# Context of chunks 1 to 3 loaded by columns and masked in place, in an attention and expert kernel on one core

## Chip, cores and metric

The kernel runs on one core of one Trainium2 chip. The metric is the device time of one execution in microseconds (us), lower is better; each kernel is run several times and the median counts.

## What is computed

One layer over 32 sequences of 64 tokens with 128 features, in fp32: cross-attention with 8 heads against a context, a small feed-forward part, and a mixture of 16 routed experts (the best 2 of 4 groups, then the best 4 experts) with two shared ones.

```python
q = einsum('bsd,hdk->bhsk', layernorm(x), Wq);  k = einsum('btd,hdk->bhtk', ctx, Wk);  v = ...(ctx, Wv)
A = m * (q @ k.T) + (1 - m) * -1e30;            o = softmax(A) @ v
y = layernorm(ctx + o @ Wo) * g0 + b0
x = x + layernorm(y + relu(y @ W1 + b1) @ W2 + b2) * g1 + b1'
h = layernorm(x)
combine = route(h @ router_w.T)                 # sigmoid, 2 groups of 4, 4 experts, weights normalised, x 2.5
out = x + sum_e combine_e * (silu(h @ gate_e) * (h @ up_e)) @ down_e + shared(h)
```

## The kernel before

The 2048 tokens are 16 tiles of 128, in four chunks (`c` = 0 to 3) of four tiles (512 tokens). Each engine has its own list of pieces (`key(c, h)`, `scores(n)`, `gate(n)`, ...), written out by hand as calls. The engines run their lists in that order and meet only at semaphores, so the order of the calls is the schedule. From `up(42)` on the lists are loops.

Wq and Wk of each head are folded into one matrix at the start (`fold` on PE, `centre` and `fold_low` on DVE, `fold_high` on ACT). What was folded is then multiplied by the context. `key(c, h)` makes the keys of chunk `c` and head `h` with three single-pass matmuls of 128x512: the operands are split into a high part (a copy rounded to fp32r) and a low part (the residue), and high x high, high x low and low x high are added in PSUM. Of the context, chunk `c` therefore needs features on partitions, times the mask, split in two:

- `mask_context(c)` (POOL, lines 430 to 440) multiplies the context by rows, `ctx_all`, by the mask of each token into `ctx_m`;
- `turn_ctx(c)` (PE, lines 1498 to 1507) turns the four tiles of `ctx_m` with transposes into PSUM bank `key_bank[0]`;
- `cT_high(c)` (ACT) casts the bank to `cT_hi`, `cT_low(c)` (DVE) takes bank minus `cT_hi` into `cT_lo`;
- then `key(c, 0)` to `key(c, 7)`, whose results ACT copies to `k_T` (`key` on ACT).

`scores(n)` multiplies a tile of x by the keys (bank 4), DVE applies mask and scale (`mask`, `maximum`), POOL subtracts the maximum, ACT takes the exponent, DVE sums, POOL normalises, `turn_probs` and `spread` turn the probabilities, `attend` multiplies the context by them, `heads_out` copies, `project` applies the folded Wv and Wo, and `add_ctx` adds the context. `turn_x1`, `ffn_up`, `ffn_down` are the feed-forward part of a chunk, `turn_xm` and `route` its router logits.

The routing is done in two halves of eight tiles. DVE works from `bias_scores` to `combine`; `turn_combine` turns the weights on PE, `take_combine` copies them, SP stores them to DRAM and loads each expert's row, broadcast to 128 partitions. `weigh(n)` on POOL multiplies an expert's activations by it. `up(n)` is six matmuls (gate and up, three each) for step `n`, that is one expert and one chunk; `down(n)` adds its result to the chunk's sum in PSUM. The first weighted step is 4.

All large loads but the first ones are issued by SP in one queue (lines 332 to 361): x of chunk 0, context of chunk 1, `mask_add` (the additive mask, two transfers of 256 KB), the second half of the attention weights, `ctx_swap`, the remaining rows and columns of x and the context, small weights, and, once the folds are done, the gate and up weights in three batches and the down weights. PSUM bank 0 serves `turn_ctx` and the even heads, counted by `key_use` and `ctx_use`.

Of the kernel before, what the change touches and what calls it, by code (L numbers as in the profile page):

```python
# [57 lines left out]
def build(nc, x, x_cols, ctx_in, mask_tok, mask_pairs, w_attn, w_gu, w_dn, small, w1, w2, vec, out):  # L58
    es = ExitStack()
    with es:  # L60
# [23 lines left out]
        ctx_m = sb("ctx_m", [P, TPC, P])  # L84
        mask_col = sb("mask_col", [P, NT])
# [114 lines left out]
        ld_c0, ld_c1, ld_c = sem("ld_c0"), sem("ld_c1"), sem("ld_c")  # L200
        ld_mask_col, ld_mask, ld_swap0, ld_swap = sem("ld_mask_col"), sem("ld_mask"), sem("ld_swap0"), sem("ld_swap")
# [17 lines left out]
        cT_hi_ready = sem("cT_hi_ready")  # L219
# [26 lines left out]
        def ctx_use(c):  # L246

            return c * (1 + HP) + 1

        def key_use(c, h):  # L250

            return ctx_use(c) + 1 + h // 2 if h % 2 == 0 else c * HP + h // 2 + 1

# [65 lines left out]
        def _(sp):  # L319
# [15 lines left out]

            sp.wait_ge(ld_w[0][1], 16)
            rows(0, 1, ld_x0)
            context(1, 2, ld_c1)
# [7 lines left out]
            columns(1, 2, ld_xt[1])  # L346
            context(2, CH, ld_c)
# [45 lines left out]
        def _(pool):  # L393
# [36 lines left out]
            def mask_context(c):  # L430

                if c < 3:
                    pool.wait_ge((ld_c0, ld_c1, ld_c)[c], 16)
                if c == 0:
                    pool.wait_ge(ld_mask_col, 16)
                else:
                    pool.wait_ge(key_full[0], ctx_use(c - 1))
                now = slice(c * TPC, (c + 1) * TPC)
                pool.tensor_tensor(ctx_m[:], ctx_all[:, now, :], mask_col[:, now].unsqueeze(2)
                                   .to_broadcast([P, TPC, P]), ALU.mult).then_inc(ctx_m_ready, 1)  # L440
# [70 lines left out]
            subtract_max(0)  # L511

            subtract_max(1)
            mask_context(2)
            normalise_probs(0)
            inverse_root(0, 1)
            normalise_probs(1)

            subtract_max(2)

            subtract_max(3)
            normalise_probs(2)
            add_beta(0)
            group_order()
            inverse_root(0, 2)
            normalise_probs(3)
            mask_context(3)

            subtract_max(4)

            subtract_max(5)
            normalise_probs(4)
            bias_row_2()

            subtract_max(6)
            split_lo(0)
            normalise_probs(5)
            add_beta(1)

            subtract_max(7)  # L540
            normalise_probs(6)
            inverse_root(0, 3)
            add_beta(2)
            inverse_root(1, 0)

            subtract_max(8)

            subtract_max(9)
            normalise_probs(7)
            add_b2(0)  # L550

            subtract_max(10)
            split_lo(1)
            normalise_probs(8)
            split_lo(2)
            inverse_root(2, 0)

            subtract_max(11)
            normalise_probs(9)
            inverse_root(3, 0)  # L560
            normalise_probs(10)
            add_beta(3)
            inverse_root(1, 1)

            subtract_max(12)
            normalise_probs(11)

            subtract_max(13)
            add_b2(1)

            subtract_max(14)
            normalise_probs(12)

            subtract_max(15)
            normalise_probs(13)
# [3 lines left out]
            split_lo(3)  # L579
            inverse_root(3, 1)  # L580
            split_lo(4)
            split_lo(5)
            inverse_root(1, 2)
            add_b2(2)
            dn_low(0)
            inverse_root(1, 3)
            split_lo(6)
            dn_low(1)
            inverse_root(2, 2)
# [5 lines left out]
            weigh(9)  # L595
            weigh(10)
            weigh(11)
            add_b2(3)
            weigh(12)
            weigh(13)  # L600
            weigh(14)
            weigh(15)
            inverse_root(3, 2)
            inverse_root(2, 3)
            weigh(16)
            weigh(17)
            weigh(18)
            weigh(19)
            weigh(20)
            dn_low(2)  # L610
            weigh(21)
            weigh(22)
            inverse_root(3, 3)
            weigh(23)
            weigh(24)
            split_lo(7)
            weigh(25)
            weigh(26)
            weigh(27)
            weigh(28)  # L620
# [3 lines left out]
            weigh(31)  # L624
            weigh(32)
            weigh(33)
            dn_low(3)
            weigh(34)
            weigh(35)
            weigh(40)  # L630
            weigh(41)
            weigh(42)
            weigh(43)
            weigh(44)
            weigh(45)
            weigh(46)
            weigh(47)
            weigh(48)
            weigh(49)
            weigh(50)  # L640
            weigh(51)
            weigh(52)
            weigh(53)
            weigh(54)
            weigh(55)
            weigh(56)
            weigh(57)
            weigh(58)
            weigh(59)
            weigh(60)  # L650
            weigh(61)
            weigh(62)
            weigh(63)
            weigh(64)
            weigh(65)
            weigh(66)
# [1345 lines left out]
```

## Time and profile before

| | us |
|---|---|
| median of 3 runs | 298.83 (298.77 to 298.99) |
| profiled execution | 299.21 |
| its span | 297.4 |
| PE busy | 284.9 (96%) |
| POOL busy | 182.9 (61%) |
| DVE busy | 179.6 (60%) |
| ACT busy | 161.7 (54%) |
| HBM read / written | 27.54 MB / 1.18 MB |

The span is the time from the first to the last instruction. PE's busy time counts matmuls, and their ends are modelled, so neighbours overlap a little; the chain of waits shows them end to start. The granted clock of PE was 0.998 over the execution. The loads fall in the first 33 us, in which the 16 DMA engines are busy nearly all the time from 14 us on.

### The profile page before, as it was taken

How to read it: one execution, taken by the hardware profiler on the slowest of the kernel's cores; microseconds unless marked ns; L12 is line 12 of the kernel's file. 1: busy time of each engine (PE TensorE's matmuls, PEld its weight loads, DVE VectorE, ACT ScalarE, POOL GpSimd, SP SyncE). 2: the span in 40 equal slices, each digit the busy share in tenths (PEclk: the TensorE clock that was granted, in tenths of full speed). 3: DMA queues.
4: the chain of work that ended last, by engine and by line, in shares of the span. 5: the costliest groups of instructions: out<-in, count | busy, mean ns of one | idle time of the engine just before them, and what ended most of it. 6: DMA issues, size and time to landing. Idle time of an engine off the chain costs nothing.

```text
span 297.4 us, 4503 instructions
## 1 busy us (share of the span) xinstructions
PE 284.9 (96%) x1427; PEld 206.9 (70%) x1427; DVE 179.6 (60%) x476; ACT 161.7 (54%) x298; POOL 182.9 (61%) x167
## 2 busy tenths in 40 slices
PE   2999999999999999999799999999999999999995
PEld 2756568757786787866666766767668888888882
DVE  0747855656755686796173427358965756566561
ACT  2555857574776677863342544573254564545541
POOL 2148686855576466342566966846706787877881
PEclk9999999999999999999999999999999999999999
DMA  6799300003000001101752432320045246334101
GB/s 210 244 361 297 128 0 3 0 2 100 7 2 0 3 1 57 51 0 45 264 185 82 141 124 90 129 83 3 1 151 193 90 141 210 116 100 142 71 2 71
DMA packets 9575, 29.01 MB, mean 98 GB/s; under 512 B 1232, under 2 KB 2256, under 8 KB 9424
## 3 DMA queue, kind: packets, MB, share of 16 engines
q1 hardware_dynamic: 8688, 27.15, 27.2%
q10 hardware_dynamic: 864, 1.57, 1.6%
q8 instruction: 12, 0.20, 0.3%
q14 instruction: 11, 0.09, 0.1%
HBM read 27.54 MB, written 1.18 MB: 97 GB/s over the span
## 4 chain that ended last, share of the span: by engine, by line
PE 86%; DVE 5%; DMA 4%; POOL 2%; issue 2%; ACT 0%; DVEq 0%; POOLq 0%
PE bank L1494 15%; PE bank L1495 15%; PE bank L1496 15%; PE bank L1573 10%; PE bank L1700 9%; PE bank L1561 6%; PE bank L1533 5%; PE bank L1542 3%; PE bank L1595 2%; PE bank L1602 2%; DMA k_T<-comb_dram 2%; POOL k_T L497 2%; DMA ctx_all<-in_ctx_in 1%; PE bank L1624 1%; DMA comb_dram<-comb_T 1%
## 5 line engine op out<-in xcount | busy, mean ns | idle before, releaser
L497 POOL TENSOR_TENSOR k_T<-x_T,k_T 128x512 f32<-128x512 f32 x64 | 94.0, 1475 | 44.8 <-DVE x_T L1274 34.7
L789 ACT ACTIVATE x_T<-bank 128x512 f32<-128x512 f32 x72 | 42.9, 597 | 68.4 <-PE bank L1496 68.3
L1274 DVE TENSOR_TENSOR x_T<-bank,x_T 128x512 f32<-128x512 f32 x64 | 44.1, 690 | 53.2 <-ACT x_T L789 29.5
L1494 PE MATMUL bank<-mT_hi,we_hi 128*128 128x512 f32 x144 | 62.5, 434 | 0.0
L1495 PE MATMUL bank<-mT_lo,we_hi 128*128 128x512 f32 x144 | 56.9, 395 | 0.0
L1496 PE MATMUL bank<-mT_hi,we_lo 128*128 128x512 f32 x144 | 56.8, 395 | 0.0
L1700 PE MATMUL bank<-k_T,w_in 128*128 128x512 f32 x78 | 36.6, 595 | 1.8 <-POOL k_T L497 1.8
L1494 PEld LDWEIGHTS bank<-mT_hi,we_hi 128*128 128x128 f32 x144 | 27.1, 188 | 9.1 <-issue 3.5
L1495 PEld LDWEIGHTS bank<-mT_lo,we_hi 128*128 128x128 f32 x144 | 27.1, 188 | 8.2 <-issue 2.9
L1573 PEld LDWEIGHTS bank<-vo,o_T 128*128 128x128 f32 x256 | 30.2, 192 | 2.3 <-issue 2.0
L1496 PEld LDWEIGHTS bank<-mT_hi,we_lo 128*128 128x128 f32 x144 | 27.0, 188 | 6.5
L1573 PE MATMUL bank<-vo,o_T 128*128 128x128 f32 x256 | 31.6, 276 | 0.0
L419 POOL TENSOR_TENSOR sc_m<-sc_m,nmax 128x512 f32<-128x512 f32 x16 | 17.1, 1070 | 15.1 <-DVE nmax L1130 15.1
L403 POOL TENSOR_TENSOR rstd<-var_eps,neg_half 128x4 f32<-128x4 f32 x12 | 12.4, 1032 | 21.9 <-DVE var_eps L1093 21.8
L720 ACT COPY o_T<-bank 128x512 f32<-128x512 f32 x32 | 17.9, 591 | 14.6 <-PE bank L1561 14.5
L1700 PEld LDWEIGHTS bank<-k_T,w_in 128*128 128x128 f32 x78 | 14.3, 190 | 13.8 <-issue 11.0
L1279 DVE TENSOR_TENSOR act_lo<-k_T,act_hi 128x512 fp32r<-128x512 f32 x33 | 22.8, 692 | 1.2 <-ACT act_hi L798 1.2
L691 ACT COPY k_T<-bank 128x512 f32<-128x512 f32 x32 | 18.5, 590 | 7.6 <-PE bank L1496 6.8
L798 ACT CAST act_hi<-k_T 128x512 fp32r<-128x512 f32 x33 | 20.2, 616 | 4.4 <-POOL k_T L497 2.4
L427 POOL TENSOR_TENSOR prob<-sc_m,rsum 128x512 f32<-128x512 f32 x16 | 16.7, 1046 | 7.2 <-DVE rsum L1137 5.9
L1123 DVE SCALAR_TENSOR_TENSOR sc_m<-bank,rstd_in,mask_add 128x512 f32<-128x512 f32 x16 | 11.9, 744 | 13.7 <-PE bank L1533 11.4
L1561 PE MATMUL bank<-prob_T,ctx_all 64*128 64x256 f32 x64 | 18.1, 402 | 0.0
(127 smaller groups left out, 488.1 us busy)
## 6 DMA issues: line engine op xcount, KB each, us to landing
k_T<-comb_dram SPq DMA_DIRECT2D x32, 512.0 KB, 3.7
w_in<-in_w_gu SPq DMA_DIRECT2D x3, 768.0 KB, 4.4
w_in<-in_w_dn SPq DMA_DIRECT2D x1, 1152.0 KB, 9.7
w_in<-in_w_attn ACTq DMA_DIRECT2D x4, 256.0 KB, 4.8
w_in<-in_w_attn SPq DMA_DIRECT2D x2, 512.0 KB, 7.5
ctx_swap<-in_ctx_in SPq DMA_DIRECT2D x2, 384.0 KB, 12.0
out_x<-ctx_all SPq DMA_DIRECT2D x3, 256.0 KB, 4.6
x_all<-in_x SPq DMA_DIRECT2D x2, 256.0 KB, 5.7
```

Source lines behind the costliest of these rows:

```text
L497: pool.tensor_tensor(act[n % 4], s_u[n % 2], comb[u % RING][:, c % 2 * CW:(c % 2 + 1) * CW], ALU.mult).then_inc(weighed_ready, 1)
L691: a.copy(k_T[c % 2][:, :, h, :], key_bank[i][:].rearrange("p (b s) -> p b s", s=SEQ)).then_inc(key_free[i], 1)
L789: a.activation(silu[n % 2], h_bank[n % 2][:], ACT.Silu).then_inc(silu_ready, 1)
L798: a.copy(act_hi[n % LAG][:], act[n % 4]).then_inc(act_hi_ready, 1)
L1274: v.tensor_tensor(into, u_bank[n % 2][:], silu[n % 2], ALU.mult).then_inc(s_u_ready, 1)
L1279: v.tensor_tensor(act_lo[n % LAG][:], act[n % 4], act_hi[n % LAG][:].bitcast(F32), ALU.subtract).then_inc(act_lo_ready, 1)
L1494: pe.matmul(dst, w_hi, m_hi, start=start, stop=False)
L1495: pe.matmul(dst, w_hi, m_lo, start=False, stop=False)
L1496: return pe.matmul(dst, w_lo, m_hi, start=False, stop=stop)
L1561: last = pe.matmul(o_bank[j][:].rearrange("p (h b s) -> p h b s", b=2, s=SEQ)[:, :, s, :], held[rows, n, :], prob_T[n % 2][rows, :, s, :], ...
L1573: last = pe.matmul(av_bank[:, 0:P], o_T[n % 2][:, h % 2, h // 2, :], vo[:, h, :], start=(h == 0), stop=(h == NH - 1))
L1700: pe.matmul(acc[c][:], dn[:, e, :], act[n % 4], start=start, stop=stop).then_inc(down_full, 1)
```

## The change

Chunk 0 is handled as before. For chunks 1 to 3 the host lays out the context a second time by columns (`ctx_cols`), and the mask as one row of 2048 (`mask_row`). SP loads for each of them 512 columns of the context into one tile `ctx_t` (256 KB) and the mask row, broadcast to 128 partitions, into `mask_r` (256 KB). `mask_context` multiplies `ctx_t` by `mask_r` in place; `cT_high` and `cT_low` read `ctx_t` instead of the bank. `turn_ctx(1)` to `(3)` are gone. The context by rows is still loaded for all chunks; chunk 1's comes later in the queue. A semaphore `cT_ready` frees `ctx_t` and `mask_r` for the next chunk, and SP waits for it before the loads of chunks 2 and 3.

Besides, the lists of all five engines are in another order. `mask_rows` stands ahead of `mask_context(1)` on POOL, most `turn_probs`, `attend` and `project` stand earlier, `attend(15)` stands between `turn_xm(1)` and `route(1)`, `project(15)` right behind `project(14)`, `up(5)` behind `turn_combine(0)`, `turn_combine(1)` behind `down(33)`, `combine(0)` and `combine(1)` one DVE piece or more earlier, and the loops start at step 42 on all engines, with `dn_high(4)` and `dn_low(4)` ahead of them. The core of the diff; of the lists only the parts on which the text below rests:

```diff
+        ctx_t, mask_r = sb("ctx_t", [P, CW]), sb("mask_r", [P, CW])
+        ld_cols = [None] + [sem(f"ld_cols{i}") for i in range(1, CH)]
...
+            def context_columns(c):
+
+                now = slice(c * CW, (c + 1) * CW)
+                if c > 1:
+                    sp.wait_ge(cT_ready, c - 1)
+                sp.dma_start(mask_r[:], mask_row[now].partition_broadcast(P)).then_inc(ld_cols[c], 16)
+                sp.dma_start(ctx_t[:], ctx_cols[:, now]).then_inc(ld_cols[c], 16)
+
             sp.wait_ge(ld_w[0][1], 16)
             rows(0, 1, ld_x0)
-            context(1, 2, ld_c1)
+            context_columns(1)
...
             columns(1, 2, ld_xt[1])
+            context(1, 2, ld_c1)
             context(2, CH, ld_c)
...
             sp.dma_start(small_T[:], small).then_inc(ld_small, 16)
+            context_columns(2)
             sp.wait_ge(fold_done, 6)
...
                     sp.dma_start(dn, w_dn).then_inc(ld_dn, 16)
+                    context_columns(3)
...
             def mask_context(c):
-                if c < 3:
-                    pool.wait_ge((ld_c0, ld_c1, ld_c)[c], 16)
-                if c == 0:
-                    pool.wait_ge(ld_mask_col, 16)
-                else:
-                    pool.wait_ge(key_full[0], ctx_use(c - 1))
...
+                if c:
+                    pool.wait_ge(ld_cols[c], 32)
+                    pool.tensor_tensor(ctx_t[:], ctx_t[:], mask_r[:], ALU.mult).then_inc(ctx_m_ready, 1)
+                    return
...
             mask_context(0)
+            mask_rows()
             mask_context(1)
             inverse_root(0, 0)
-            mask_rows()
...
-                a.copy(cT_hi, key_bank[0][:]).then_inc(cT_hi_ready, 1)
+                a.copy(cT_hi, ctx_t[:] if c else key_bank[0][:]).then_inc(cT_hi_ready, 1)
...
-                v.tensor_tensor(cT_lo[:], key_bank[0][:], cT_hi.bitcast(F32), ALU.subtract).then_inc(key_free[0], 1)
+                v.tensor_tensor(cT_lo[:], ctx_t[:] if c else key_bank[0][:], cT_hi.bitcast(F32), ALU.subtract
+                                ).then_inc(cT_ready if c else key_free[0], 1)
...
             def key(c, h):
...
-                if h < 2:
-                    pe.wait_ge(key_free[0], ctx_use(c))
+                if c and h < 2:
+                    pe.wait_ge(cT_ready, c)
...
             key(0, 7)
-            turn_ctx(1)
             fold(1, 0)
...
             turn_xm(1)
+            attend(15)
             route(1)
             project(14)
-            attend(15)
+            project(15)
+            turn_x1(2)
             up(2)
...
             ffn_up(2, 0)
+            ffn_up(2, 1)
+            up(4)
...
             down(1)
             down(2)
-            ffn_down(2)
-            up(4)
+            turn_combine(0)
+            down(3)
+            turn_x1(3)
             up(5)
-            turn_combine(0)
...
```

## Rows read from the trace of the kernel before

**Rows 1.** The page, first part: TensorE's busy time, share of the span, instructions.

```profile
PE 284.9 (96%) x1427; PEld 206.9 (70%) x1427; DVE 179.6 (60%) x476; ACT 161.7 (54%) x298; POOL 182.9 (61%) x167
```

**Rows 2.** Waits of PE: waiter, what it waited for, total us, times, longest.

```profile
PE bank L1506 <- POOL ctx_m L439: 5.7, 1, 5.7
PE bank L1700 <- POOL k_T L497: 1.8, 1, 1.8
PE bank L1624 <- ACT xm_T L752: 0.7, 1, 0.7
PE bank L1652 <- DVE comb_w L1254: 0.6, 1, 0.6
```

**Rows 3.** Chain that ended last: start us, us, engine, tile, line, instructions.

```profile
16.64 0.64 PE bank L1506 x4
...
20.77 1.01 PE bank L1533 x4
...
28.50 0.44 PE bank L1506 x4
...
33.37 1.06 PE bank L1561 x8
...
45.78 1.79 PE bank L1573 x16
...
49.77 1.98 PE bank L1573 x16
```

**Rows 4.** Busy time by stretch: us, PE, PEld, DVE, ACT, POOL, clock, DMA share, GB/s.

```profile
22.00:24.00 2.00, 2.00 (x14) 1.79 (x14) 1.93 (x4) 1.10 (x2) 0.60 (x1) 1.00 1.07 259
...
28.00:30.00 2.00, 2.00 (x15) 1.16 (x13) 0.41 (x1) 1.20 (x4) 1.45 (x2) 1.00 1.04 423
```

**Rows 5.** The two loads of `mask_add`: issue ns, first and last start, landing.

```profile
L340 SPq DMA_DIRECT2D mask_add<-in_mask_pairs x2: 517/554/590, 7.8 to 8.4; - x2
...
DMA to landing us min/median/max: 4.9/5.4/6.0
```

**Rows 6.** Timeline of POOL, 11 to 19 us: start, us, engine, line, operation, tiles.

```profile
11.90 1.04 POOL L439 TENSOR_TENSOR ctx_m<-ctx_all,mask_col 128x512 f32<-128x512 f32 x1 [6.35 <-DMA ctx_all<-in_ctx_in]
...
17.05 1.04 POOL L464 TENSOR_SCALAR mask_add<-mask_add 128x1024 f32<-128x1024 f32 x1
```

**Rows 7.** Timelines of ACT, DVE and PE, 17 to 20 us.

```profile
17.31 0.59 ACT L683 CAST key_room<-bank 128x512 fp32r<-128x512 f32 x1
...
17.93 0.69 DVE L1112 TENSOR_TENSOR cT_lo<-bank,key_room 128x512 fp32r<-128x512 f32 x1 [2.08 <-ACT key_room L683]
...
19.11 0.50 PE L1494 MATMUL bank<-key_room 128*128 128x512 f32 x1
...
19.91 0.40 PE L1494 MATMUL bank<-key_room 128*128 128x512 f32 x1
```

**Rows 8.** Timelines of DVE and POOL, 210.5 to 212.5 us.

```profile
210.72 1.70 DVE L1151 TENSOR_TENSOR mT_lo<-xm_T,mT_hi 128x512 fp32r<-128x512 f32 x1
...
210.60 1.26 POOL L497 TENSOR_TENSOR k_T<-x_T,k_T 128x512 f32<-128x512 f32 x1 [2.17 <-issue]
```

**Rows 9.** Issues of two loads by SP, and their us to landing (page, part 6).

```profile
17.32 0.43 SPq L354 DMA_DIRECT2D small_T<-in_small  x1
...
23.96 0.43 SPq L361 DMA_DIRECT2D w_in<-in_w_dn  x1
...
w_in<-in_w_dn SPq DMA_DIRECT2D x1, 1152.0 KB, 9.7
...
small_T<-in_small SPq DMA_DIRECT2D x1, 64.0 KB, 11.7
```

**Rows 10.** Chain that ended last, around the first half's combine weights.

```profile
136.88 2.65 DMA comb_dram<-comb_T
139.54 5.04 DMA k_T<-comb_dram
...
146.06 1.12 PE bank L1700 x2
```

More of the change, by code:

```diff
@@ L609, in _ @@
             weigh(20)
-            dn_low(2)
+            split_lo(7)
             weigh(21)
             weigh(22)
+            weigh(23)
             inverse_root(3, 3)
-            weigh(23)
             weigh(24)
-            split_lo(7)
             weigh(25)
@@ L619, in _ @@
             weigh(27)
+            dn_low(2)
             weigh(28)
@@ L624, in _ @@
             weigh(31)
+            dn_low(3)
             weigh(32)
             weigh(33)
-            dn_low(3)
             weigh(34)
             weigh(35)
+            dn_low(4)
             weigh(40)
             weigh(41)
[L632 to L656, printed above, removed]
-            weigh(67)
-            weigh(68)
-            dn_low(4)
-            for n in range(69, N):
+            for n in range(42, N):
                 if weighted(n):
@@ L952, in _ @@
             heads_out(14, 1)
+            gate(0)
             normalise(3, 1)
@@ L987, in _ @@
             gate(17)
+            dn_high(4)
+            gate(18)
             normalise(3, 2)
-            gate(18)
             take_xm(2)
@@ L1308, in _ @@
             sum_of_exp(0)
-            statistics(0, 1)
-            sum_of_exp(1)
             mask(2)
             maximum(2)
+            statistics(0, 1)
+            mask(3)
+            sum_of_exp(1)
+            sum_of_exp(2)
+            statistics(0, 2)
+            maximum(3)
             cT_low(2)
-            mask(3)
-            maximum(3)
-            sum_of_exp(2)
             mask(4)
-            statistics(0, 2)
+            maximum(4)
+            add_ctx(0)
             mask(5)
             sum_of_exp(3)
-            maximum(4)
+            sum_of_exp(4)
             maximum(5)
@@ L1372, in _ @@
             maximum(12)
+            sum_of_exp(11)
+            add_ctx(8)
             mask(13)
+            maximum(13)
             take_logits(0)
-            add_ctx(8)
-            maximum(13)
             mask(14)
             maximum(14)
-            mT_low(0)
             sum_of_exp(12)
+            mask(15)
             add_ctx(9)
             sum_of_exp(13)
-            mask(15)
+            sum_of_exp(14)
+            mT_low(0)
+            add_ctx(10)
             maximum(15)
-            add_ctx(10)
-            sum_of_exp(14)
             add_ffn(1)
@@ L1406, in _ @@
             group_scores(0)
+            add_ctx(15)
             keep_groups(0)
-            add_ctx(15)
+            statistics(1, 3)
             gate_up(2)
-            statistics(1, 3)
             keep_experts(0)
+            combine(0)
             gate_up(3)
-            combine(0)
             add_ffn(2)
             take_combine(0)
+            statistics(2, 2)
             gate_up(4)
-            statistics(2, 2)
             gate_up(5)
@@ L1811, in _ @@
             attend(9)
+            project(8)
+            turn_xm(0)
             turn_probs(10)
-            turn_xm(0)
-            project(8)
+            scores(13)
             route(0)
-            scores(13)
             attend(10)
@@ L1872, in _ @@
             down(6)
+            down(7)
+            down(8)
             up(11)
             up(12)
-            down(7)
-            down(8)
+            up(13)
+            up(14)
             down(9)
@@ L1892, in _ @@
             down(16)
-            up(20)
+            down(17)
             up(21)
```

410 lines of the change are left out of this document (189 added, 221 removed).

## Prediction

> **What bounds the kernel now.** I read the page's first part, then the list of what TensorE (PE) waited for, then the chain of waits, and last the timelines of the other engines where PE had waited. PE is busy 284.9 us of a span of 297.4 [rows 1]. Its order is written out by hand, and once the first folds are through the chain is nearly all PE: a piece starts when the one before it ends. The list of waits [rows 2] holds the exceptions that this case turns on (two more, 0.5 us in the tail and 0.2 early, are untouched): 5.7 us at the start for the first masked context, 1.8 us for the first weighing of a routed expert, 0.7 us for a copy between two neighbouring pieces, 0.6 us for the second set of routing weights. So a PE piece that goes is worth its length, and an edit on another engine or queue is worth nothing unless it makes PE wait or ends one of these waits. Two such places can be bad: the first 35 us, where the loads fill the DMA engines, and the routing of each half, whose chain crosses DVE, PE, DMA and GpSimd (POOL).
>
> The profiled execution took 299.21 us with a span of 297.4, so 1.8 us lie outside the span; I leave them as they are. The median of the runs shown is 298.83. All steps below are differences in the span, and I take them off the median.
>
> **What goes: three `turn_ctx`.** The chain has 0.64 us for the first of them and 0.44 for the second; the third also has 0.44 [rows 3]. The dearer one carries a wait for bank 0 at its head. PE has no other cover there, so the sum is 0.64 + 0.44 + 0.44 = 1.5 us. The changes of type beside them partly stay with their neighbours, so I take 1.4, between 1.2 and 1.5.
>
> **What the new order costs PE itself.** All other pieces stay, but not their neighbours. A `project` takes 1.79 us after most pieces and 1.98 after `scores` [rows 3], so leaving a `scores` or `attend` costs the next piece some 0.15 to 0.2. In the order of before, `scores` or `attend` is followed by another kind of piece 24 times, in the new one 26 times: 2 x 0.17 = 0.3 us more, between 0 and 0.4.
>
> **The first chunk's columns.** Before, `turn_ctx(1)` and the fold stood on PE between `key(0,7)` and `scores(0)`; now the chain is mask rows landed, `mask_rows`, `mask_context(1)`, cast, residue, `key(1,0)`. On SP's queue, `context_columns(1)` puts 512 KB where 256 KB of context stood, and `mask_add`, the second attention weights and all behind them are moved by 256 KB. The DMA engines moved 259 GB/s in a stretch of 2 KB rows and 423 in one of longer rows [rows 4]; at 259 GB/s 256 KB are 1.0 us, at 423 they are 0.6. I take 0.9, since both new tiles have 2 KB rows. `mask_add` landed at 8.4 + 6.0 = 14.4 us [rows 5], so now at 15.3. POOL does `mask_rows` (1.04) and then `mask_context(1)` (1.04) [rows 6]: 17.4. The cast takes 0.59 on ACT, the residue 0.69 on DVE [rows 7], with some 0.1 for the hand-over: 18.75. PE would be there at 18.6, which is the 19.11 of before [rows 7] less the turn. That is a wait of 0.15 us, if nothing collides. One thing can. The residue used to read a PSUM bank and now reads two SBUF tiles, as `mT_low` does, and that one took 1.70 us at 210.72 when a POOL multiply of 1.26 had begun at 210.60 [rows 8]. It ended 0.56 after POOL's. `inverse_root(0,0)` now runs on POOL just behind `mask_context(1)`, when `cT_low(1)` is due. By this row each of the three residues can take 0 to 1.0 us longer. I take 0.4 us for the first chunk in all, between 0 and 0.9. DVE's own queue behind it holds `mask(0)`, which PE's `scores(1)` waits for, so this wait isn't made good later.
>
> The Trainium skill (SBUF — State Buffer, Who interferes with whom) says that a DVE instruction with two SBUF inputs contends with a GpSimd instruction that reads SBUF, and that the second to start fully blocks. By that rule, the trace agrees: 1.70 against 0.69. Taken strictly for all three residues it would add up to 3.0 us and leave a gain near zero; I don't take it so, since the third has slack and the row shows only the rest of POOL's instruction being waited out.
>
> **The second chunk's columns.** `context_columns(2)` is issued behind `small_T`, whose landing was 17.3 + 11.7 = 29.0 us [rows 9]. Ahead of it are now 512 KB more (0.5 MB of new tiles, no load less), and it is 512 KB itself: 1 MB at 259 to 423 GB/s is 2.5 to 4.0 us, so it lands between 31.5 and 33.0; I take 32.4. POOL 1.04, ACT 0.59, DVE 0.69 and hand-overs of 0.15 make it ready at 34.9. When does PE want it? From `key(1,0)` at 19.1 there stand before `key(2,0)` eight keys of 0.70 (three matmuls; 0.80 from 19.11 to 19.91 with the change of type [rows 7]), four `scores` of 1.01, two `attend` of 1.06, one `project` of 1.98, three turns of four of 0.44 [rows 3], a fold of 0.8, and some eight changes of type at 0.1: 5.6 + 4.0 + 2.1 + 2.0 + 1.3 + 0.8 + 0.8 = 16.6, so 35.7 at most and 35.1 if most changes are hidden. That is a margin of 0.2 to 0.8 us, and a late landing or a blocked residue (up to 1.0) eats it: 0 to 1.3 us, I take 0.4. While POOL waits for this load, `subtract_max(3)` is queued behind it, and while DVE waits for the residue, `mask(4)`; their users on PE come 4 us later or more, so they cost nothing by themselves.
>
> **The third chunk's** pair is issued behind the down weights, which landed at 24.0 + 9.7 = 33.7 before [rows 9] and come some 3 us later now. `key(3,1)` stands near 57 us, with `project(3)`, `attend(4)`, a turn and `scores(8)` (4.4 us) after `key(2,7)`, whose end frees the high part. Nothing. The loads behind (`vec_row`, `w1_in`, the gate and up batch) come 1.6 to 4 us later; their users stand at 36 us or later. Nothing. The context by rows for chunk 1 goes behind `x_T`, with its first reader, `attend(4)`, near 54 us. Nothing. SP's new waits on `cT_ready` hold back only loads with that slack.
>
> **The stretch from 35 to 117 us.** Before, PE didn't wait in it at all. The new order has no neighbours there that pass a tile through another engine, so I take 0, between 0 and 0.8.
>
> **Routing of the first half.** PE waited 0.7 for `xm_T` between `turn_xm(1)` and `route(1)` [rows 2]; `attend(15)` (1.06) now stands between and hides it. `up(5)`, two keys long or 1.4 us, moves from before `turn_combine(0)` to behind it. Against that, two pairs have become neighbours that need another engine in between: `project(14)`/`project(15)` (the bank must be taken by `add_ctx`, and the copy of o_T stands behind the sigmoid: 0.45) and `ffn_up(2,0)`/`ffn_up(2,1)` (an ACT eviction like the 0.59 of [rows 7] and hand-over: 0.75). `gate(0)` now stands ahead of `normalise(3,1)` on ACT: 0.2. So `turn_combine(0)` comes 0.7 + 1.4 - 0.45 - 0.75 - 0.2 = 0.7 us earlier by the waits alone, and a second count, piece by piece from `turn_xm(1)`, gives 1.05 (the wait and the missing change of type). From there the rest is a chain of fixed length: store 2.65, load 5.04, `weigh(4)`, first weighted `down` at 146.06 [rows 10]. It moves by the same amount, and PE, with 1.4 us more to do meanwhile, waits some 0.5 instead of 1.8. `combine(0)` on DVE also moves ahead of `gate_up(3)`, so the weights are ready by then. Gain 1.0, between 0 and 1.9.
>
> **Routing of the second half.** PE waited 0.6 for `comb_w` [rows 2]. Now `combine(1)` stands two or three DVE pieces earlier, `mT_low(3)` behind it, and `turn_combine(1)` behind `down(33)`. The wait goes: 0.6, between 0.3 and 0.6. What is late next is the load of the combine weights, whose user stands 10 us later. The last 70 us keep PE's order. `dn_low(4)` and `dn_high(4)` move to an earlier place where PE has a queue of ready work: nothing.
>
> **Sum.** -1.4 + 0.3 + 0.4 + 0.4 + 0 - 1.0 - 0.6 = -1.9 us: 298.83 - 1.9 = 296.9.
>
> **Rivals.**
> Everything in time: no wait at 19 and 35 us, and the routing chain short enough that PE hardly waits at 146. -1.4 + 0.3 - 1.6 - 0.6 = -3.3: 295.5. For it speaks that both margins are near zero rather than negative; against it that two new tiles per chunk go through a full DMA queue. Chance 0.20.
> The routing chain doesn't shorten: ACT or DVE reaches the softmax statistics or `combine(0)` no earlier, because PE's gain of the first 117 us isn't matched there. -1.4 + 0.3 + 0.4 + 0.4 + 0 - 0.6 = -0.9: 297.9; with an 0.8 us wait in the middle stretch 298.7. For it speaks that PE waited for ACT at that place already [rows 2], so the two arrive close together. Chance 0.23.
> On the slower side, late columns for chunk 2: if they don't land in the order of issue but together with the gate, up and down weights issued from 24 us on, they are there at 33.7 + 3.2 = 36.9 us, `key(2,0)` at 36.9 + 2.5 = 39.4, and PE waits 4.0 us instead of 0.4: 296.9 + 3.6 = 300.5. It decides from a landing later than some 34.7 us. Against it speaks that `small_T`, issued 6 us ahead of these weights, landed at 29.0, and the down weights, issued last, landed last, at 33.7 [rows 9]. The Trainium skill (DMA: Bandwidth & Descriptors, Queues, rings and completion order) says that each engine takes descriptors in ring order but that completion is not first in, first out for an issuing engine; the landings shown here don't contradict either half. Chance 0.10.
>
> **How the numbers follow.** The forecast holds 0.47, for 296.2 to 297.6. The range must leave out no more than 0.2: I cut the far half of the first rival and the late columns, 295.2 to 298.8. A measurement of this kernel can tell some 0.2% (0.6 us) from no change. Faster by more than that, below 298.2: 0.47 + 0.20 + 0.12 of the second rival = 0.79. Within it: 0.09. Slower: 0.12, the late columns and a little of the middle stretch.
>
> **What would show it.** The matmul count falls by 12, to 1415. Steps right: PE's first `key(1,0)` near 19 us with a wait under 0.5; `key(2,0)` between 35 and 36; the wait before line 1700's first weighted `down` near 0.5 and not 1.8; no wait for `comb_w`; residues of 0.7 to 1.7 us. Wrong: new rows in PE's list of waits between 20 and 117 us, a `ctx_t` that lands after 34 us, or the same 1.8 us in front of that `down`.

## The result, and the profile after

The changed kernel takes 299.38 us (median of 21 runs), the kernel before 298.48 (21 runs). The ratio is 1.0037, 95% interval 1.0025 to 1.0048: slower by 0.9 us by the medians and 1.1 by the ratio (0.7 to 1.4), where 1.9 us less was forecast.

The page of the changed kernel, first part; it answers to [rows 1]:

```profile
span 297.3 us, 4482 instructions
PE 285.0 (96%) x1415; PEld 206.7 (70%) x1415; DVE 176.6 (59%) x476; ACT 160.6 (54%) x298; POOL 185.9 (63%) x167
```

The twelve transposes are gone (1415 matmuls for 1427), and PE's busy time hasn't fallen. The waits of PE in the changed kernel (waiter, what it waited for, total us, times, longest) answer to [rows 2]:

```profile
PE bank L1466 <- POOL ctx_m L446: 5.6, 1, 5.6
PE bank L1557 <- ACT hid L726: 0.8, 1, 0.8
PE bank L1457 <- DVE x_T L1237: 0.8, 1, 0.8
PE bank L1457 <- DVE cT_lo L1074: 0.5, 1, 0.5
PE bank L1535 <- DVE ctx_all L1104: 0.5, 1, 0.5
PE bank L1670 <- ACT o_T L794: 0.5, 1, 0.5
PE bank L1602 <- DMA w_in<-in_w_attn: 0.2, 1, 0.2
PE bank L1457 <- DVE key_room L1126: 0.2, 1, 0.2
```

The three waits of before (1.8, 0.7 and 0.6) are gone, as forecast. New are 0.8 between the two `ffn_up(2)`, 0.8 within `up(33)`, 0.5 at `key(1,0)`, 0.5 between `project(14)` and `project(15)`, 0.2 at the first fold. (The 0.5 for `o_T` in the tail and the 0.2 for `key_room` are those of before.)

The two profiles alone can't explain the result: the span is 297.3 against the 297.4 of before, so by them nothing was lost, while the medians differ by 0.9. The profiled execution of before (299.21) lay 0.7 above its own median. So the experiments had two questions: what each part does, and what that one execution had that the others have not. The second turned out to matter more.

### The profile page after: what moved, and what is told of

Read it like the earlier page. It is cut to its first block, busy times and chain, and to the rows that moved or that the text cites. A ratio compares the mean times of both kernels' runs of the same rounds, so it can differ in the third digit from the quotient of the medians.

```text
span 297.3 us, 4482 instructions
## 1 busy us (share of the span) xinstructions
PE 285.0 (96%) x1415; PEld 206.7 (70%) x1415; DVE 176.6 (59%) x476; ACT 160.6 (54%) x298; POOL 185.9 (63%) x167
## 4 chain that ended last, share of the span: by engine, by line
PE 87%; DMA 4%; DVE 4%; ACT 1%; issue 1%; POOL 1%; SPq 1%; ACTq 0%; DVEq 0%
PE bank L1457 16%; PE bank L1458 15%; PE bank L1459 15%; PE bank L1535 10%; PE bank L1662 10%; PE bank L1523 6%; PE bank L1493 5%; PE bank L1502 3%; DMA mask_add<-in_mask_pairs 2%; PE bank L1557 2%; PE bank L1564 2%; DMA w_in<-in_w_attn 2%; PE bank L1586 1%; PE bank L1550 1%; PE bank L1577 1%
## 5 line engine op out<-in xcount | busy, mean ns | idle before, releaser
L435 POOL TENSOR_TENSOR prob<-sc_m,rsum 128x512 f32<-128x512 f32 x16 | 16.6, 1044 | 9.9 <-DVE rsum L1100 9.6
```

## Experiments

The median of before was between 298.1 and 298.4 in all of these. Times by piece are starts of the same PE piece in each profiled execution; each kernel but the one before has only one of these, so a difference of some tenths early in the span can be chance.

**The column layout without the new order.** In before's order of pieces (in short, not the code itself):

```diff
+            context_columns(1), (2), (3)      # where the change has them
-            turn_ctx(1), turn_ctx(2), turn_ctx(3)
```

> The kernel before with the column layout alone: context columns and mask rows loaded for chunks 1 to 3, no turns of the context, every list in the order of before. Theory A (the order made room for the loads): key(2,0) stands at 30.7 us in that order and the second chunk's columns land near 32, so PE waits some 4 us before key(2,0), and POOL's subtract and normalise pieces are held up behind mask_context(2); 3 times 0.45 us of turns goes: about 301.5 us. Theory B (the layout is harmless and all of the loss is in the order): 298.5 - 1.4 = 297.1 us, with no wait before key(2,0).

Measured: 308.46 us, ratio 1.033 (1.030 to 1.036), slower than both theories had it (about 301.5 and 297.1). PE's first row of waits in it, and busy time by stretch (us, PE, PEld, DVE, ACT, POOL, granted clock, DMA share, GB/s):

```profile
PE bank L1549 <- POOL prob L435: 6.2, 1, 6.2
...
28.00:35.00 7.00, 0.95 (x3) 0.45 (x3) 0.32 (x2) 1.21 (x2) 2.14 (x2) 0.72 1.06 380
35.00:38.00 3.00, 2.82 (x8) 1.01 (x8) 0.67 (x1) 1.56 (x3) 3.00 (x4) 0.50 0.57 150
38.00:41.00 3.00, 3.00 (x11) 2.49 (x10) 2.23 (x4) 1.66 (x3) 1.68 (x3) 0.50 0.46 102
```

`normalise_probs(0)` stands behind `mask_context(2)` in POOL's old order, and that waits until 32.9 us for its load; `turn_probs(0)` then waits 6.2 us on PE. After this idle stretch the granted clock is 0.50 (1.2 GHz) for 6 us (35 to 41), and the matmuls pay a second time; in before it is 1.00 there. So the layout needs a new order on POOL; this part of the order isn't free choice.

**The new order without the layout.** The turns and loads of before in the changed kernel's order, with `turn_ctx(2)` right behind `key(1,7)`:

> The changed kernel with the turns put back (turn_ctx behind key(c,7)) and the loads of before: only the order differs from the kernel before. Theory A (the order itself costs PE at the start, by fold(0,3) moved away and the slow matmuls after it, about 1 us, and at the second routing about 0.4 net): 298.5 + 0.3 (changes of type) + 1.0 + 0.4 - 1.8 (first routing) = 298.4 us. Theory B (order good, loads bad): 298.5 + 0.3 - 1.8 = 297.0 us.

Measured: 300.84 us, 1.009 (1.0073 to 1.0107). This is not a clean half: PE waits for a masked context twice, 7.3 us in all of which 5.8 are the wait at the start, so some 1.5 us fall on `turn_ctx(2)`.

```profile
PE bank L1459 <- POOL ctx_m L439: 7.3, 2, 5.8
```

The new order has POOL's `mask_context(2)` behind `subtract_max(2)` and `normalise_probs(2)` too. So its total says little about the order. Two of its stretches do, since neither has to do with the layout or with the new arrays, which this kernel doesn't declare: from `turn_xm(1)` to `down(4)` it takes 27.71 us and from `down(4)` to `up(39)` 74.60, as the changed kernel (27.74 and 74.62). What happens in the two routings comes from the order.

**`fold(0, 3)` back ahead of the first keys.**

```diff
             fold(0, 2)
+            fold(0, 3)
             key(0, 0)
             key(0, 1)
-            fold(0, 3)
```

> The changed kernel with fold(0,3) back in front of key(0,0) on PE. Theory A (PE stood idle in the place of this fold, and its first six key matmuls then took 0.43 us each instead of 0.23): the first keys run at 0.23 us from start to start again, key(0,2) starts near 11.5 us instead of 12.9, and the time falls by 0.5 to 1.2 us to 298.2 to 298.9. Theory B (the slow matmuls come from late weights of the first folds, whatever the order): first keys as slow as before this edit, 299.4 us.

Measured: 299.42 us, 1.0039 (1.0025 to 1.0053). The second to sixth matmul of the keys start 0.23 us apart again, where three of them are 0.43 apart in the changed kernel. But PE waits 1.5 us for `w_in` (0.5 at the first fold, 1.1 for the second attention weights), and `key(1,0)` starts at 21.06. No gain: in this execution the loads set this stretch. The slow spacing isn't the fold's place alone either: it comes in 0 to 5 of these matmuls, in before's order too (5 in the kernel below with two arrays that nobody reads, 1 in the second execution of before). Two neighbours in the changed kernel, and two in the kernel with the layout alone, where the granted clock was 0.50:

```profile
11.08 0.63 PE L1459 MATMUL bank<-key_room 128*128 128x512 f32 x1
11.51 0.63 PE L1457 MATMUL bank<-key_room 128*128 128x512 f32 x1
...
39.90 0.63 PE L1506 MATMUL bank<-key_room 128*128 128x512 f32 x1
40.32 0.63 PE L1504 MATMUL bank<-key_room 128*128 128x512 f32 x1
```

So these first matmuls go at the pace of the lower clock (1.2 GHz), though the profile has 1.00 for this stretch. Each costs 0.2 us; why there are more of them in one execution than in another stays open.

**The columns of chunk 1 masked first.** POOL does `mask_context(1)` and `inverse_root(0, 0)` ahead of `mask_rows`.

> The changed kernel with mask_context(1) and inverse_root(0,0) ahead of mask_rows on POOL, as before. Theory A (the columns of chunk 1 land before mask_add, and waiting for mask_add first costs PE's wait for key(1,0)): mask_context(1) starts near 14 us, key(1,0) starts right behind scores(0), the PE wait of 0.6 us there goes, mask(0) then waits for mask_rows to end near 18 us without hurting: 298.8 us. Theory B (the columns land as late as mask_add, so the order on POOL doesn't matter): 299.4 us.

Measured: 299.35 us, 1.0037 (1.0019 to 1.0054). `key(1,0)` follows `scores(0)` without a wait, at 20.36, but the first weights came late in that execution. The 0.5 us wait is real, but the median doesn't move with it.

**Chunk 1 turned on PE again**, chunks 2 and 3 by columns:

```diff
-            context_columns(1)
+            context(1, 2, ld_c1)
...
             key(0, 7)
+            turn_ctx(1)
```

> The changed kernel with chunk 1 handled as in the kernel before: context by rows loaded in its old place, masked, turned on PE; POOL in its old order for the first four pieces; only chunks 2 and 3 by columns, so SP's queue is the old one up to small_T. Theory A (the loss of 1.6 us up to key(1,0) comes from the 256 KB more and the one more transfer ahead of mask_add and the second attention weights, and from the chain through the masks): key(1,0) back near 19.5 to 20 us (the slow matmuls around fold(0,3) remain), plus 0.5 for the turn that is back in it: 298.3 to 298.9 us. Theory B (the late start is the scatter of the first weights' landing and the slow matmuls, not the queue): 299.4 + 0.5 = 299.9 us.

Measured: 299.37 us, 1.0042 (1.0027 to 1.0056), between the two theories; `key(1,0)` at 20.70, with a turn ahead of it, where the changed kernel has 20.74 without one. By the medians, taking the chunk's columns away brings nothing back. The kernel also has POOL's first pieces in the order of the experiment before, so it isn't the columns alone that changed.

**Two `down` between `up(33)` and `up(34)`**, for the wait within the tail of the second routing:

> The changed kernel with up(34) behind down(29) and down(30) on PE. Theory A (PE waits 0.8 us before up(34) for gate_up(32), which DVE does late because its group_scores and keep_groups wait behind POOL's multiplies; PE itself has other work to do meanwhile): the wait goes, and nothing behind it in the kernel holds PE back again, so the span falls by 1.0 us: 299.4 to 298.4 us. Theory B (DVE is behind for longer, and PE only waits elsewhere, at up(35) or at down(31)): 299.4 us.

Measured: 299.51 us, 1.0049 (1.0028 to 1.0071). I had misplaced the wait: it is inside `up(33)`, whose second half wants the buffer that `gate_up(31)` frees. The timeline of the changed kernel (start, us, engine, line, operation) and then, in a second execution of before, the same DVE addition and two later operations of the routing:

```profile
196.00 1.27 POOL L494 TENSOR_TENSOR dn_lo<-w_in,key_room 128x512 fp32r<-128x512 f32 x1
197.24 1.33 POOL L504 TENSOR_TENSOR k_T<-x_T,k_T 128x512 f32<-128x512 f32 x1
197.46 1.23 DVE L1166 TENSOR_TENSOR k_T<-k_T 128x96 f32<-128x96 f32 x1
198.53 1.30 POOL L484 TENSOR_TENSOR we_lo<-w_in,we_hi 128x512 fp32r<-128x512 f32 x1
198.61 1.33 DVE L1167 TENSOR_TENSOR k_T<-k_T 128x64 f32<-128x64 f32 x1
206.46 0.50 PE L1457 MATMUL bank<-mT_hi,we_hi 128*128 128x512 f32 x1 [0.76 <-DVE x_T L1237]
```

```profile
195.71 0.26 DVE L1203 TENSOR_TENSOR k_T<-k_T 128x96 f32<-128x96 f32 x1
...
200.31 1.35 DVE L1217 TENSOR_TENSOR k_T<-k_T 128x128 f32<-128x128 f32 x1
201.69 1.26 DVE L1218 TENSOR_TENSOR k_T<-k_T,lower 128x128 f32<-128x128 f32 x1
```

The small additions of the group scores (0.26 and 0.24 us) take 1.23 and 1.33, and each ends 0.1 us after the POOL instruction that had begun just before it. It is the behaviour of [rows 8] at a place where I hadn't looked; POOL's new order puts `dn_low(2)`, a weighing and `split_lo(8)` there. This needn't be the whole cause of the wait. Before has two such long operations as well, a little later. And in the new order of PE, `route(3)` stands at 194.07 us and not at 190.93, so that the group scores begin 1.65 us later (196.66 for 195.01), while `up(33)` is only 0.34 later. No run has the one without the other.

**Routing of the first half rearranged**: `up(2)` between `project(14)` and `(15)`, `up(4)` between the two `ffn_up(2)`, `turn_combine(0)` ahead of `down(1)`.

> The changed kernel with up(2) between project(14) and project(15), up(4) between the two ffn_up of chunk 2, and turn_combine(0) ahead of down(1) and down(2) on PE. Theory A (these pairs cost 0.6 and 0.9 us, and the combine weights were ready on DVE 2 us before PE turned them, so their chain can move with PE): both waits go, the first weighted down comes 1.5 us earlier with no wait before it: 297.9 us. Theory B (the chain of the combine weights has a fixed end near 145.7 us, whatever PE does): PE waits there, and the time stays at 299.4 us.

Measured: 299.48 us, 1.0045 (1.0031 to 1.0059). Both waits go, and others come, as PE's waits in it show:

```profile
PE bank L1457 <- DVE x_T L1237: 0.7, 1, 0.7
PE bank L1457 <- DVE k_T L1237: 0.6, 1, 0.6
PE bank L1457 <- ACT x_T L771: 0.5, 1, 0.5
```

The routing weights are turned 1.7 us earlier (134.99 for 136.65), yet `down(4)` starts at 145.80 for 145.74. No wait for a weighing is left, so in this kernel the weights' chain no longer sets that point; PE's own work and its waits for evictions do.

**Four of these together** (fold back, chunk 1 turned with its order on POOL, both rearrangements):

> The three edits together, and fold(0,3) back in front of key(0,0). If each cause is a term of its own and PE's order decides: the changed kernel's 299.4 less 1.0 (second routing) less 1.5 (first routing) less 1.0 (start) = 295.9 us, below both kernels. If the terms cover for each other: 297 us or more.

Measured: 298.84 us, 1.002 (1.0008 to 1.0033). By the medians about half of the loss is gone; the interval still overlaps that of the changed kernel (1.0025 to 1.0048). In the profiled execution it is gone ahead of `key(1,0)` (20.18 for 20.74), not in the two routings (27.81 and 74.60 us), so no cause that the single edits had shown accounts for it.

**The kernel before, unchanged, a second profiled execution.**

> The kernel before, unchanged, for a second profiled execution of it. The first had 299.21 us in all with a span of 297.4, while its median over the later runs is 298.2 to 298.5; every variant of the changed kernel had its profiled execution within 0.3 us of its median. Theory A, the first profiled execution of before was long by some 0.8 us at its front (first weights, fold, first keys), where the landing of the first loads differs from run to run: then the new one has a span of 296.2 to 296.8, and the 0.8 us are missing before the piece key(1,0), which starts at 18.3 to 18.6 us and not at 19.11. Theory B, the difference lies outside the span: the span is 297.3 to 297.5 again, key(1,0) again at 19.1, and in all 298.3 to 298.6. Theory C, it is spread over the later stages: key(1,0) at 19.1, but the first weighted down on PE at 145.3 or earlier.

Measured: 298.31 us, 1.0002 (0.9991 to 1.0013), span 296.7. The span is the one of theory A, but its cause is not: `key(1,0)` starts later (20.00 for 19.11), and `down(4)` earlier (145.32 for 146.06), which is theory C but for the 20.00. The chain of waits around the routing weights, to be held against [rows 10]:

```profile
137.79 2.26 DMA comb_dram<-comb_T
...
140.06 3.78 DMA k_T<-comb_dram
...
145.32 1.12 PE bank L1700 x2
```

Store and load take 6.04 us and not 7.69, 1.3 of the difference in the load and 0.4 in the store. PE's list of waits has no row for the first weighing any more. Six executions with before's order around this place, this one among them, have 6.04 to 6.64 us (3.78 to 4.32 for the load), and PE waits there between nothing and 0.7 us. The 1.8 us of [rows 2] came of one long load and a store at the long end of its spread.

**Only the last chunk by columns**, in before's order:

```diff
+            context_columns(3)      # behind w_dn
-            turn_ctx(3)
```

> Before's order of pieces on every engine, and only the last chunk of the context is laid out by columns and masked in place; chunks 0 to 2 are turned on PE as before, so that no extra byte is in the queue ahead of the second half of the loads. Theory A (the removed turn is a gain of its length where the columns are there early): 0.44 us less than before, 297.9 against 298.3, ratio 0.9985, and PE has no wait at key(3,1); all milestones from project(3) on 0.4 to 0.5 us earlier. Theory B (the removed turn is given back, since PE waits for ACT's and DVE's copies or for the routing chain anyway): down(4) at the same time as in before within 0.1 us, ratio 0.9995 to 1.0005.

Measured: 298.88 us, 1.002 (1.0005 to 1.0035): slower, by neither theory. By piece against the second execution of before: `key(1,0)` +0.73, `key(2,0)` +0.72, `project(3)` +0.29 and +0.34 at the end. The turn is worth its 0.44 us, and it is kept to the end. But 0.7 us are lost before 21 us, where no instruction differs and no load has been added. PE's second row of waits says what is late there:

```profile
PE bank L1653 <- DMA w_in<-in_w_attn: 0.7, 1, 0.7
```

**Three moves on PE, layout of before:**

```diff
             turn_xm(1)
+            attend(15)
             route(1)
             project(14)
-            attend(15)
...
             up(4)
-            up(5)
             turn_combine(0)
             turn_x1(3)
             down(3)
+            up(5)
...
-            turn_combine(1)
             down(33)
+            turn_combine(1)
```

> Before's layout and order, with three moves on PE alone: attend(15) between turn_xm(1) and route(1), up(5) from before turn_combine(0) to behind down(3), and turn_combine(1) behind down(33). Theory A (the three waits of before, 0.7 for xm_T, 1.8 for the first weighing and 0.6 for comb_w, can be had by PE's order alone): 0.7 us by route(1), and down(4) earlier by 1.0 to 1.8 us in all, the end by 1.3 to 2.2: 296.1 to 297.0, ratio 0.993 to 0.996. Theory B (comb_w is not ready earlier, since ACT's softmax statistics and DVE's combine stand behind other work there): PE waits at turn_combine(0) for as long as up(5) was, down(4) moves by 0.3 us at most, and what is left is 0.3 to 0.6 from the second half: 297.7, ratio 0.998.

Measured: 297.14 us, 0.9964 (0.9952 to 0.9976), faster than the kernel before and the changed one. By the profiled execution nearly all of it is the last move: `down(4)` at 145.35 against 145.32, `up(39)` at 218.95 against 219.81. In the first half theory B holds: what `route(1)` gained PE waits for again at `turn_combine(0)`.

```profile
PE bank L1652 <- DVE comb_w L1254: 1.0, 1, 1.0
```

**Both together:**

> Both of the two before: last chunk by columns and the three moves. Theory A (each gain is PE time and they add): the gains of chunk3_only and routes_only add up within 0.1 us, 295.6 to 296.6, ratio 0.991 to 0.994. Theory B (both go into the same wait in front of the first weighted down): the time of routes_only within 0.1 us.

Measured: 297.55 us, 0.9982 (0.9964 to 0.9999). The two ratios together would give 0.9984, so they add, loss included (theory A had left the loss out).

**The kernel before with the two new arrays declared and read by nobody:**

```diff
-        ... ctx_in=tiles(ctx_1024), mask_tok=...
+        ... ctx_in=tiles(ctx_1024), ctx_cols=..., mask_row=..., mask_tok=...
```

> The kernel before, instruction for instruction, with the two new input arrays of the change (ctx_cols, 1 MB, and mask_row, 8 KB) declared between ctx_in and mask_tok and read by nobody. In the four profiled executions without these arrays the first fold starts at 6.57 to 6.74 us and never waits for its weights; in the ten with them it starts at 6.93 to 7.56 and mostly waits for them, though the loads issued before it are the same, and the move rate between 4.5 and 5.7 us is 70 to 190 GB/s in several of them. Theory A (the arrays' presence, by where it puts the others in memory or otherwise, slows the first loads): first fold at 7.0 or later, key(1,0) at 20.5 or later and not at 20.0, median 0.4 to 0.7 us over before, ratio 1.0015 to 1.0025, though no instruction differs. Theory B (it is the queue: later loads of the changed kernels, or chance): first fold at 6.6 to 6.8, ratio 0.999 to 1.001.

Measured: 299.23 us, 1.0031 (1.0016 to 1.0046). Not one instruction differs from before, and it is 1.1 us slower: theory A, and more than the 0.4 to 0.7 us it had. The profiled execution (300.10) is the slowest of the twelve, so its times by piece (first fold at 7.41 us, `key(1,0)` at 21.09) are an extreme. Four executions of this PE order without the array in the middle have `key(1,0)` between 18.94 and 20.00, a spread that no array explains. Busy time from 4.5 to 6.0 us (columns as above), in the second execution of before, in this kernel, and in the changed one:

```profile
4.50:6.00 1.50, 0.14 (x1) 0.18 (x2) 0.00 (x0) 0.41 (x1) 1.04 (x1) 1.00 0.83 266
```

```profile
4.50:6.00 1.50, 0.44 (x2) 0.47 (x3) 0.00 (x0) 0.41 (x1) 0.91 (x1) 1.00 0.81 158
```

```profile
4.50:6.00 1.50, 0.40 (x2) 0.43 (x3) 0.00 (x0) 0.42 (x1) 0.96 (x1) 1.00 0.69 180
```

The same loads are under way in this stretch, and they move 158 to 180 GB/s in place of 266; in the middle row at the same DMA share (0.81 for 0.83), in the last at a lower one. This row splits all executions here without an overlap: with `ctx_cols` declared ahead of the weights, 156 to 213 GB/s (12 kernels) and a first fold at 6.93 to 7.56 us; otherwise 266 to 326 GB/s (8 executions) and a first fold at 6.47 to 6.74. The DMA share is lower too, 0.58 to 0.82 for 0.83 to 1.02, but by less than the rate.

**The same two arrays, declared last:**

> The kernel before, instruction for instruction, with the two new input arrays declared behind all others and read by nobody. Theory A1 (what costs time is where the arrays of before lie, and only those behind the inserted ones are shifted): first fold at 6.4 to 6.8 us, ratio to before 0.998 to 1.001. Theory A2 (each further array costs time by itself, wherever it lies): ratio 1.002 to 1.0045 as with inputs_only (1.0031).

Measured: 298.41 us, 1.0003 (0.9992 to 1.0015), first fold at 6.54, 270 GB/s. Theory A1: what counts is that the arrays are declared ahead of others, not that there are more.

**Only the 8 KB array, declared in the middle:**

> The kernel before, instruction for instruction, with only mask_row (8 KB) declared between ctx_in and mask_tok and read by nobody. If the small array's shift of all that is declared behind it is what hurts: first fold later than 6.9 us, ratio 1.002 to 1.004. If it is the 1 MB array, or the count of two: first fold at 6.6 to 6.8, ratio 0.999 to 1.001.

Measured: 298.32 us, 1.0005 (0.9989 to 1.002), first fold at 6.73. So it is the 1 MB array in the middle (or both together), not the small one by itself.

**The changed kernel with both arrays last, and with the small one last:**

> The changed kernel with the two new arrays declared behind all others, so that the arrays of before are declared in the order of before. Theory A with placement as the mechanism: first fold at 6.6 to 6.8 us, the changed kernel 0.3 to 0.6 us faster than it was, ratio to before 1.0015 to 1.0025 in place of 1.0037. Theory A with another mechanism (each further array costs start-up time), or theory B: first fold at 6.9 to 7.5, ratio 1.003 to 1.0045.

> The changed kernel with ctx_cols (1 MB) where it was and mask_row (8 KB) declared behind all others. If the small array's shift hurts: first fold at 6.4 to 6.8 us, key(1,0) near 20.0 and not 20.7, and ratio to before 1.000 to 1.0025 in place of 1.0037. If not: first fold at 6.9 to 7.5, ratio 1.003 to 1.0045.

Measured: 300.18 us, 1.0066 (1.0045 to 1.0087), and 301.26 us, 1.0097 (1.0075 to 1.0119). Both went against me. With both last the first fold is early (6.47), but PE then waits 2.1 us for `w_in`, most of it for the second attention weights; with the small one last it waits 2.9. The changed kernel reads these arrays itself, so their place decides about more than the first loads. Which place suits which load, no run shows; nor does any show what the arrays cost in the changed kernel.

**The best of all:** chunk 3 by columns, the three moves, both arrays last.

> chunk3_routes (before's order, last chunk by columns, the three moves on PE) with the two new arrays declared behind all others. By placement: first fold at 6.6 to 6.8 us, and the turn that was removed is at last seen in the time: 0.4 us below routes_only, 296.7 against 298.2, ratio 0.995. Otherwise 297.4 to 297.6 again, ratio 0.998.

Measured: 296.84 us, 0.9954 (0.9941 to 0.9966), first fold at 6.48: 1.3 us faster than before, 2.5 faster than the changed kernel. Its instructions are those of the kernel with chunk 3 and the moves (297.55); only the place of the arrays differs. So here too the place in the middle costs time, 0.7 us by the medians (the intervals of the two ratios just touch), in a kernel that reads one chunk of them.

## Why the prediction was wrong

**The turns, -1.4: right.** `turn_ctx(3)` alone is worth 0.43 (+0.72 at `key(2,0)`, +0.29 at `project(3)`). Between `key(1,0)` and `project(3)` the changed kernel gains 0.91 us on the second execution of before, for two turns.

**Changes of type and the middle stretch, +0.3 and 0: right.** From `project(3)` to `turn_xm(1)` the changed kernel loses 0.39 us, and PE's list of waits has no row there.

**The first chunk's columns, +0.4: right in kind and about in size, on a wrong base.** The timeline of the changed kernel:

```profile
16.91 1.05 POOL L471 TENSOR_SCALAR mask_add<-mask_add 128x1024 f32<-128x1024 f32 x1 [11.45 <-DMA mask_add<-in_mask_pairs]
18.04 1.27 POOL L442 TENSOR_TENSOR ctx_t<-ctx_t,mask_r 128x512 f32<-128x512 f32 x1
19.34 0.62 ACT L665 CAST key_room<-ctx_t 128x512 fp32r<-128x512 f32 x1 [0.76 <-POOL ctx_t L442]
19.99 0.69 DVE L1074 TENSOR_TENSOR cT_lo<-ctx_t,key_room 128x512 fp32r<-128x512 f32 x1 [3.86 <-ACT key_room L665]
20.74 0.50 PE L1457 MATMUL bank<-key_room 128*128 128x512 f32 x1 [0.54 <-DVE cT_lo L1074]
```

The chain is the one worked out, with a wait of 0.54 us where the term had 0.4. But it starts at 16.9 and not at 15.3: `mask_add` landed 1.6 us later than I had it. I took 1.04 us for a mask that multiplies two whole tiles; it takes 1.27. The residue wasn't blocked: 0.69. Against the kernel with the same arrays declared, `key(1,0)` is 0.35 us earlier (20.74 for 21.09), where my terms (-0.64 + 0.4) make 0.24; these are single executions, and over the four variants with the same columns and arrays it lies between 20.36 and 21.23. Against the two of before it is 0.7 to 1.6 later.

**The second chunk's columns, +0.4: too dear.** They were masked at 33.3, some 0.9 later than forecast, and the residue (0.87) was done by 36.2, but `key(2,0)` came at 37.60 and not at 35.1 to 35.7, since PE itself was later (16.9 us after `key(1,0)`, for 16.0 to 16.6). It didn't wait. The rival of late columns, the one I had on the slower side, is refuted: slower came by another way.

**Routing of the first half, -1.0: this step failed.** Its small terms came in: 0.5 between the two `project` for 0.45, 0.8 between the two `ffn_up` for 0.75, the wait for `xm_T` gone. But the gain was to come out of the 1.8 us of [rows 2], and these rest on one load of 5.04 us [rows 10]. With 3.8 to 4.3 there are 0 to 0.7 us to be had. What I had counted up to the turn of the weights was right: from `turn_xm(1)` to `turn_combine(0)` it is 18.65 us for 19.38, 0.7 less. But PE's own work and waits then fill the time to `down(4)`. From `turn_xm(1)` to `down(4)` the changed kernel takes 27.74 us, and so do seven variants with these pieces in the same order (27.71 to 27.73). Before's order takes 27.54 to 28.14 in six executions, by the load, and 29.18 in the one that I had. So the step is worth between +0.2 (against the second execution of before) and -0.4, -0.2 against the middle of the six, and not -1.0. My second rival (the chain doesn't shorten) had the right consequence with the wrong mechanism: the chain was short already.

**Routing of the second half, -0.6: given back.** The wait for `comb_w` goes, and `up(33)` waits 0.8 us for DVE. From `down(4)` to `up(39)` it is 74.62 us for 74.49: +0.1. That the move itself is good shows in the three moves alone: 73.60. I had asked whether the weights come in time and not what the new lists do to DVE ahead of them. Long additions beside POOL and the later `route(3)` both delay it; their shares aren't shown.

**What no term had: the arrays.** I costed the added loads by their bytes and never asked what two more arrays do to the loads already there. That is +1.1 us (1.0016 to 1.0046 as a ratio) in the kernel that has nothing else, and 0.7 by the pair with one chunk by columns.

**What I left as it is: the time outside the span.** It is 2.1 us in the changed kernel and 1.8 in both executions of before. Nine of the ten kernels that load two or three chunks by columns have 1.93 to 2.13 (the tenth 1.77), all ten other executions 1.72 to 1.85. So some 0.2 to 0.3 us go with the column loads; by what, is open.

Put together: -1.9, +0.8 to +1.2 for the first routing, +0.7 for the second, -0.4 for the second chunk, +1.1 for the arrays and some +0.2 outside the span make +0.5 to +0.9 us; measured 0.9 by the medians. This sum treats the arrays' cost as one that adds to the rest, and the changed kernel got slower and not faster with the arrays last (1.0066), so it shows that the sizes fit and not that each is paid in this kernel. Also open is why the place of an array changes the rate of the first loads.

The Trainium skill (SBUF — State Buffer, Who interferes with whom) says that of a DVE instruction with two SBUF inputs and a GpSimd instruction that reads SBUF the second to start is blocked. By that rule, the trace agrees in the group scores: 1.23 and 1.33 us for 0.26 and 0.24. I had weighed it at the three residues, where it cost nothing or 0.2 us, and not at the pieces that POOL's new order put side by side.

## What to carry to other kernels

Before a gain is taken out of a wait that ends in a DMA, profile the old kernel again: one long load made 1.8 us of a wait that is 0 to 0.7, and the spans of the two profiles then agreed by accident. When a change adds an input array, time the old kernel with that array declared and unused; here it gave 1.0031 by itself. Try the array's place in the changed kernel as well: the best place for one kernel was not the best for the other. And when the order on POOL changes, compare DVE's durations line by line: here additions were longer by 1 us each, some 7 us ahead of PE's wait.

## What was not expected of the hardware

- In the twelve kernels with a 1 MB input declared between the others (in one of them read by nobody) the first loads moved 156 to 213 GB/s from 4.5 to 6.0 us, in the eight other executions 266 to 326, and the first fold came 0.2 to 1.1 us later. Declared last, the input had no such effect on them.
- The load of the routing weights took 3.78 to 4.32 us in six executions and 5.04 in one; the store ahead of it 2.25 to 2.65.
- Additions of 128x96 and 128x64 on DVE, 0.26 and 0.24 us by themselves, took 1.23 and 1.33 beside POOL's work.
- The first matmuls of the keys start 0.43 us apart instead of 0.23 in 0 to 5 cases per execution, the spacing of a granted clock of 0.50, while the profile's clock there is 1.00.
- After 6.2 us without PE work the granted clock was 0.50 for the next 6 us; without this gap it is 1.00 there.
